# A transformer block: half of the MLP's gated column groups multiplied by GpSimd in one instruction instead of by VectorE in four

## The reference, cut to what matters

```python
h = _ln(x) * (1 + sc_msa) + sh_msa
x = x + _self_attn(h, ...) * g_msa                # stage A: windows of 128 rows, 16 heads
h = _ln(x) * (1 + sc_mca) + sh_mca
x = x + _topk_cross_attn(h, context, ...) * g_mca # stage B: the best 16 of 77 keys
h = _ln(x) * (1 + sc_mlp) + sh_mlp
u = h @ w_m1 + b_m1                               # stage C: the MLP, HID = 1024
a, b = (u[..., :HID], u[..., HID:])
x = x + (jax.nn.silu(a) * b @ w_m2 + b_m2) * g_mlp
# stage D: adaptive layer norm, cross-attention over 77 keys, residual
```

## Time and profile before

| | us |
|---|---|
| median of 3 runs | 997.29 |
| lowest and highest run | 996.76, 1002.76 |
| profiled execution, whole | 996.91 |
| its span, first to last instruction | 994.8 |
| busy in the span: PE | 945.2 |
| PE weight loads | 828.5 |
| DVE | 852.7 |
| ACT | 783.6 |
| POOL | 682.9 |

### The profile page before, as it was taken

The page is one execution under the profiler, slowest core; times in us unless marked ns, Lnnn a source line. Parts: engine busy times, 40 slices in busy tenths (PEclk is TensorE's granted clock), DMA queues, the critical chain, the costliest instruction groups (busy, mean ns, idle before and its releaser), DMA issues. The chain is left out here.

```text
span 994.8 us, 32865 instructions
## 1 busy us (share of the span) xinstructions
PE 945.2 (95%) x10750; PEld 828.5 (83%) x10750; DVE 852.7 (86%) x4268; ACT 783.6 (79%) x1679; POOL 682.9 (69%) x1099
## 2 busy tenths in 40 slices
PE   6876999999999999999999999999999999998896
PEld 4655888888889899888888999988898999877784
DVE  2599898999999999999999999999999998888544
ACT  2456788888888888888888888888888888776664
POOL 1347677777777777777777777777777776766843
PEclk9999999999999999999999999999999999999999
DMA  8474200000000011100000001000100000000000
GB/s 285 119 152 74 60 18 18 23 24 23 23 18 12 18 24 23 24 23 24 23 18 12 19 24 23 23 23 23 24 8 21 20 23 18 18 8 7 7 6 18
DMA packets 72154, 33.67 MB, mean 34 GB/s; under 512 B 56520, under 2 KB 68961, under 8 KB 71346
## 3 DMA queue, kind: packets, MB, share of 16 engines
q1 hardware_dynamic: 71986, 31.57, 12.9%
HBM read 22.64 MB, written 8.91 MB: 32 GB/s over the span
## 5 line engine op out<-in xcount | busy, mean ns | idle before, releaser
L2245 PE MATMUL ps<-hT_C,w_m_sb 128*128 128x128 f32 x2048 | 266.1, 279 | 1.4 <-DVE hidden_C L1584 0.6
L2245 PEld LDWEIGHTS ps<-hT_C,w_m_sb 128*128 128x128 f32 x2048 | 248.4, 192 | 15.0 <-issue 8.6
L960 ACT ACTIVATE silu_C<-ps,cols_sb 128x128 f32<-128x128 f32 x256 | 93.6, 368 | 77.4 <-PE ps L2245 75.8
L2256 PE MATMUL ps<-w_m_sb,hidden_C 128*128 128x256 f32 x512 | 120.8, 379 | 0.0
L617 POOL TENSOR_TENSOR p_B<-p_B,rc_B 128x616 f32<-128x616 f32 x64 | 79.5, 1243 | 53.2 <-DVE p_B L1498 48.3
L1490 DVE MATCH_REPLACE8 scores_left_B<-mx_B,scores_left_B 128x77 f32<-128x77 f32 x512 | 107.7, 223 | 0.0
L1486 DVE MATCH_REPLACE8 scores_left_B<-mx_B,scores_B 128x77 f32<-128x77 f32 x512 | 107.3, 225 | 0.0
L2256 PEld LDWEIGHTS ps<-w_m_sb,hidden_C 128*128 128x128 f32 x512 | 92.5, 190 | 10.0
L1584 DVE SCALAR_TENSOR_TENSOR hidden_C<-ps,cols_sb,silu_C 128x128 f32<-128x128 f32 x256 | 83.4, 336 | 14.8 <-ACT silu_C L960 14.5
L1438 DVE TENSOR_REDUCE mx_A<-ps 128x8 f32<-128x1024 f32 x64 | 75.3, 1219 | 19.4 <-PE ps L2150 19.4
L617 POOL TENSOR_TENSOR p_D<-scores_D,rc_D 128x616 f32<-128x616 f32 x63 | 77.1, 1226 | 21.3 <-DVE rc_D L1535 15.2
(11 more groups left out here) (187 smaller groups left out, 2499.6 us busy)
## 6 DMA issues: line engine op xcount, KB each, us to landing
xn_turned<-xn_blocks_A SPq DMA_DIRECT2D x124, 32.0 KB, 2.0
xn_A<-xn_turned SPq DMA_DIRECT2D x31, 128.0 KB, 2.1
x_A<-in_x SPq DMA_DIRECT2D x28, 128.0 KB, 2.4
out<-y_D SPq DMA_DIRECT2D x28, 128.0 KB, 2.3
w_m_sb<-in_w_m SPq DMA_DIRECT2D x3, 1024.0 KB, 5.8
w_mod_sb<-in_w_mod SPq DMA_DIRECT2D x2, 1024.0 KB, 9.9
gate_b<-row_tables SPq DMA_DIRECT2D x3, 512.0 KB, 4.6
gate<-row_tables SPq DMA_DIRECT2D x2, 512.0 KB, 3.9
```

The costliest lines, as they stand in the source:

```text
L960: sc.activation(SA[:, j, :], bank(f"C.up{j}")[:, 0:P], ACT.Silu, bias=col("bm1_a", j)).then_inc(sa_ok, 1)
L2245: ins = mm(bank(f"C.up{j}")[:, half * P:(half + 1) * P], w_m1[:, k, m:m + P], HT["C"][:, t % HT_COPIES["C"], k, :], start=(k == 0), stop=( ...
L2256: ins = mm(bank("C.dn0")[:, 0:CH], G[:, t % G_COPIES, j, :], w_m2[:, j, :], start=(j == 0), stop=(j == HJ - 1))
```

## The change: what it does

Groups 0 to 3 (`DIRECT = HJ // 2`) stay as they are. For groups 4 to 7:

- the four `hidden` steps on DVE go, in fill, body and drain;
- ACT does one more instruction behind each of silu 4 to 7: an Identity activation that reads the b half from the same PSUM bank, adds its bias and writes it to a new tile UB in SBUF (4 x 128 columns, one copy); this instruction now releases the bank;
- POOL does one product SA * UB of 512 columns per tile (`multiply_rest`), which waits for all eight silus and all four copies, and whose semaphore `gp_ok` is what `down(t, 1)` now waits for. In the body it stands between `less_max` of D half 0 and `reciprocal_root` of B;
- silu 4 to 7 of the next tile wait for this product, as it reads SA and UB.

The steps that move the input of stage A through DRAM (`move_input`, `turn_input`) are rewritten so that they could serve other stages too. With `TURNED = {"A": range(1, 32)}` they issue the same transfers with the same waits, in the same place.

```diff
+DIRECT = HJ // 2
+TURNED = {"A": range(1, 32)}
+        UB = sb("gate_half_C", [P, HJ - DIRECT, P])
...
+            def multiply_rest(t):
+                pool.wait_ge(sa_ok, HJ * t + HJ)
+                pool.wait_ge(ub_ok, (HJ - DIRECT) * (t + 1))
+                if first(t):
+                    pool.wait_ge(wo_done, 2)
+                    pool.wait_ge(ct_ps, 1)
+                if t >= G_COPIES:
+                    pool.wait_ge(y_ps["C"], t + 1 - G_COPIES)
+                g.tensor_tensor(G[:, t % G_COPIES, DIRECT:, :], SA[:, DIRECT:, :], UB[:], ALU.mult).then_inc(gp_ok, 1)
...
                 run(less_max, i, 6, "D", 0)
+                run(multiply_rest, i, 5)
                 run(reciprocal_root, i, 2, "B")
                 run(less_max, i, 6, "D", 1)
...
             def silu(t, j):
                 act.wait_ge(u_ps, HJ * t + j + 1)
                 if not first(t):
-                    act.wait_ge(g_ok, HJ * (t - 1) + j + 1)
+                    if j < DIRECT:
+                        act.wait_ge(g_ok, DIRECT * (t - 1) + j + 1)
+                    else:
+                        act.wait_ge(gp_ok, t)
                 sc.activation(SA[:, j, :], bank(f"C.up{j}")[:, 0:P], ACT.Silu, bias=col("bm1_a", j)).then_inc(sa_ok, 1)
+                if j >= DIRECT:
+                    sc.activation(UB[:, j - DIRECT, :], bank(f"C.up{j}")[:, P:2 * P], ACT.Identity, bias=col("bm1_b", j)).then_inc(ub_ok, 1)
...
-                run(hidden, i, 6, 4)
                 run(select, i, 4, 3, 2)
                 run(select, i, 4, 1, 2)
-                run(hidden, i, 6, 5)
                 run(select, i, 4, 2, 3)
                 run(residual, i, 3, "A")
-                run(hidden, i, 6, 6)
                 run(statistics, i, 3, "B")
-                run(hidden, i, 6, 7)
...
-                claim(BANK[f"C.up{j}"], (g_ok, HJ * t + j + 1))
+                if j < DIRECT:
+                    claim(BANK[f"C.up{j}"], (g_ok, DIRECT * t + j + 1))
+                else:
+                    claim(BANK[f"C.up{j}"], (ub_ok, (HJ - DIRECT) * t + j - DIRECT + 1))
...
-                pe.wait_ge(g_ok, HJ * t + (half + 1) * HJ // 2)
+                if half == 0:
+                    pe.wait_ge(g_ok, DIRECT * (t + 1))
+                else:
+                    pe.wait_ge(gp_ok, t + 1)
```

More of the change, by code:

```diff
@@ L139, in block_kernel @@
         attention_work("A")
-        XB = sb("xn_blocks_A", [P, CH])
+        XB = {s: sb(f"xn_blocks_{s}", [P, CH]) for s in TURNED}
         KBa = sb("kblk_A", [P, KC, 2, P])
@@ L293, in last, with by_transfer, transfers, transposed @@
             return t == TILES - 1
+        def by_transfer(t, s):
+            return t in TURNED.get(s, ())
+        def transfers(t, s):
+            return sum(by_transfer(u, s) for u in range(t))
+        def transposed(t, s):
+            return t - transfers(t, s)
         def place(t, name):
@@ L849, in normalise @@
                 if not first(t):
-                    if s == "A":
-                        act.wait_ge(h_ok["A"], t)
+                    if by_transfer(t - 1, s):
+                        act.wait_ge(h_ok[s], t)
                     else:
-                        act.wait_ge(h_ps[s], t)
+                        act.wait_ge(h_ps[s], transposed(t, s))
                 sc.activation(XN[s][:], X[s][:, t % X_COPIES, :], ACT.Identity, scale=RS[s][:], bias=NM[s][:]).then_inc(xn_ok[s], 1)
             def modulate(t, s):
-                by_transfer = s == "A" and not first(t)
-                if by_transfer:
-                    act.wait_ge(xt_in, 16 * t)
+                if by_transfer(t, s):
+                    act.wait_ge(xt_in[s], 16 * (transfers(t, s) + 1))
                 else:
-                    act.wait_ge(h_ps[s], t + 1)
+                    act.wait_ge(h_ps[s], transposed(t, s) + 1)
                 if first(t):
@@ L1424, in statistics, with turn_input @@
                 v.bn_aggr(MV[s][:], ST[s][:, t % 2, :]).then_inc(stats[s], 1)
-            def turn_input(t):
-                dve.wait_ge(xn_ok["A"], t + 1)
-                if t > 1:
-                    dve.wait_ge(xb_out, 16 * ROWS * (t - 1))
-                v.transpose(XB[:], XN["A"][:]).then_inc(xb_ok, 1)
+            def turn_input(t, s):
+                if not by_transfer(t, s):
+                    return
+                dve.wait_ge(xn_ok[s], t + 1)
+                n = transfers(t, s)
+                if n > 0:
+                    dve.wait_ge(xb_out[s], 16 * ROWS * n)
+                v.transpose(XB[s][:], XN[s][:]).then_inc(xb_ok[s], 1)
             def maxima_a(t, c):
@@ L1702, in fill @@
                 select(2, 3, 2)
-                hidden(0, 4)
                 residual(3, "A")
                 statistics(3, "B")
-                hidden(0, 5)
-                hidden(0, 6)
                 select(2, 0, 2)
@@ L1710, in fill @@
                 select(2, 0, 3)
-                hidden(0, 7)
                 keep_chosen(2, 0)
@@ L1830, in drain @@
                 hidden(TILES - 6, 3)
-                hidden(TILES - 6, 4)
                 select(TILES - 4, 3, 3)
-                hidden(TILES - 6, 5)
                 statistics(TILES - 5, "C")
@@ L1871, in drain @@
                 hidden(TILES - 5, 3)
-                hidden(TILES - 5, 4)
                 select(TILES - 3, 3, 0)
-                hidden(TILES - 5, 5)
                 select(TILES - 3, 3, 1)
@@ L1915, in drain @@
                 statistics(TILES - 3, "C")
-                hidden(TILES - 4, 4)
                 turn_back(TILES - 1)
```

98 lines of the change are left out of this document (49 added, 49 removed).

## The result

The changed kernel is slower: 1006.22 us in the median of its 44 executions (fastest 1001.29), the kernel before 999.64 us in 139 executions beside it and beside the experiments, on five chips (fastest 996.17). The first comparison, 20 executions of each, gave a ratio of 1.0074 with a 95% interval of [1.0051, 1.0096] (medians 1006.68 and 1000.01); two later ones gave 1.0060 [1.0033, 1.0087] and 1.0054 [1.0026, 1.0082]. I had forecast 998.1 with a range of 993.0 to 1003.5; the median of the first comparison lies 3.2 us above the range, that of all 44 executions 2.7.

What follows compares the result with a forecast made beforehand. PE was taken to bound the steady part, with waits on other engines at the ends. Steady 0, fill -0.5 and drain +1.3 gave +0.8 us on 997.29, so 998.1 us, range 993 to 1003.5.

Steps and rivals of the forecast that it cites:

- What bounds the kernel: Steady part, 155 to 852 us: PE has no gap, so time taken off DVE there buys nothing by itself.
- faster throughout: Rival: PE's smooth record hides waits on DVE and the kernel follows DVE; -24 us, 973; chance 0.02.
- Banks: each of groups 4 to 7 ... Cost 0: Steady tile: ACT instead of DVE reads these banks, 0.26 us behind the silu start; up 6 and 7 get no wait.
- fall into waits for the next up: Steady tile, ACT: copies 4 and 5, 0.26 us of queue each, use time in which ACT waits anyway.
- The bound of 0.3 us a tile: Steady part: forecast cost 0, between 0 and 0.3 us a tile.
- ACT's cover: Steady tile: table load moves 0.51 us later, just covered by 0.52 us idle before key_blocks; cost 0, bounds 0 and 0.1.
- product: POOL's 512-column product: 1.28 us, bounds 0.87 and 1.55; ends 0.3 us before down half 1's weight loads; cost 0 to 0.3.
- collision: Steady tile: keep_chosen on DVE waits for the product, then reciprocal_root on POOL may wait 0.8 us for keep_chosen.
- PE sees none of it: Steady tile: add_residual moves from 508.92 to 509.3 us, POOL's next idle time takes this up, and PE loses nothing.
- The wait of 0.80 us on the maxima: Fill: PE waits for DVE's maxima behind hidden 4 to 7 of tile 0; 1.0 us less queue removes it, -0.8.
- By some 0.3 us: Fill, tile 1: the product pushes POOL's gapless chain to its weights for B; +0.3 us.
- Larger waits ... take most of it in: Drain, tiles 28 and 29: product ends 0.3 to 0.4 us late, mostly absorbed by waits for other engines; +0.2 us.

Runs made afterwards that it cites:

- e7: Kernel before without VectorE's products of groups 4 to 7, given to no other engine; median 996.92 us, ratio 0.9967.
- e4: The change in tiles 27 to 31 alone, other tiles as in the kernel before; +1.6 ± 0.8 us over the kernel before at the same clock.
- e3: The change in tiles 0 to 2 alone, other tiles as in the kernel before; +1.3 ± 0.8 us over the kernel before at the same clock.
- e2: The change in tiles 3 to 26 alone, other tiles as in the kernel before; +1.9 ± 0.8 us over the kernel before at the same clock.
- e6: Kernel before plus a 512-column GpSimd product of silu values with themselves, read by nobody; +2.0 ± 0.8 us over the kernel before at the same clock.
- e1: Changed kernel with copy 4 moved behind weights_t(D, 1) in the body; first median 1001.81 us, +4.3 ± 0.6 us over the kernel before at the same clock.

## Why the prediction was wrong, point by point

**What bounds the kernel** was right. PE sets the steady part; e7 removes 1.0 us of DVE's queue in every tile and the repeat stays at 28.08. The rival "faster throughout" did not happen.

**Steady part, predicted 0, measured +2.05 us.** The step that failed is "Banks: each of groups 4 to 7 ... Cost 0". It asked what the copies do to the banks of up 4 to 7 and not what they do to the bank that ACT releases next on its queue, bank 5, which project_o of A waits for. Bank 5 had been released in time for project_o with nothing to spare: 0.09 us later on ACT was 0.08 us later on PE, in every tile. That copies 4 and 5 "fall into waits for the next up" was true of silu 5 and not of weights_t(D, 1) in between. The bound of 0.3 us a tile did hold this value, but by another cause, a late product or copy 7; and 27 tiles of it would have been 8 us, of which the range took up only 5, at a chance of 0.10.

**ACT's cover** held: key_blocks had 0.52 us of idle time, the delay was given as 0.51, and the changed kernel leaves it 0.16 us in the body tiles, so the delay was 0.36. The **product** was sized well, 1268 ns, and no body tile waits for it. The **collision** came as told in the body. Timeline of POOL, the changed kernel run again:

```profile
540.40 1.27 POOL L657 TENSOR_TENSOR hidden_C<-silu_C,gate_half_C 128x512 f32<-128x512 f32 x1 [0.29 <-issue]
541.63 0.75 POOL L563 TENSOR_TENSOR ve_B<-mv_B,eps 128x1 f32<-128x1 f32 x1
...
544.61 0.73 POOL L667 TENSOR_TENSOR x_D<-xg_C,tmp_C 128x256 f32<-128x256 f32 x1
```

reciprocal_root's first step takes 0.75 us where it takes 0.19 elsewhere, while keep_chosen runs on DVE until 542.33:

```profile
541.14 1.19 DVE L1554 SCALAR_TENSOR_TENSOR p_B<-scores_left_B,p_B 128x616 f32<-128x616 f32 x1
```

Add_residual has lost its 1.80 us of idle time without anyone waiting for it. In this tile the two engines' steps follow each other as in the Trainium skill's account of the shared port pair (SBUF — State Buffer, "SBUF: two separate sides").

"PE sees none of it" was true of the body and not of tile 0, where the same two steps met the other way round, the product 0.09 us behind keep_chosen, so that the product ended 0.56 us later than with its usual 1.27 us. That is up to 0.56 of the 0.76 us that PE waited; no run parts the two.

**Start, predicted -0.5, measured +1.3.** Of this 0.57 us is the product of tile 0, for which the prediction had no term: it asked when POOL's product comes in body tiles, in tile 1 and in the drain. The other 0.7 lies between tile 0 and tile 3. The wait of 0.80 us on the maxima did not go away, it fell to 0.49, and gated of tile 1 does come 0.9 us sooner (25.96 for 26.85 us after tile 0), though down of that tile only 0.3 us sooner on PE. All of it is given back by the next tile, in two waits of 0.47 and 0.52 us for the weights of B on GpSimd, where before there was one of 0.19 us; GpSimd had no slack. Then the product of tile 1 pushes reciprocal_root of B: neg_mean_B ends 1.4 us later, and PE waits 0.46 us for xn_B. "By some 0.3 us" was the other mis-sized term, and a gain of DVE's was counted as one of PE's without asking whether GpSimd could follow.

**End and tail, predicted +1.3, measured +2.7** (e4 against e3, tile by tile; against e2, whose clock was full in tile 28 to 29, it would be +2.9):

| tile | predicted | measured, by gated | measured, by the start of down half 1 on PE |
|---|---|---|---|
| 27 | -0.45 | -0.39 | +0.21 |
| 28 and 29 | +0.2 | +0.73 + 0.20 | +0.03 + 0.77 |
| 30 | +0.6 | +0.66 | +0.09 |
| 31 | +0.95 | +0.96 | +0.95 |
| tail | 0 | +0.51 | |

By gated, three of the five terms are right to 0.06 us, but two of these owe that to the marker. In tiles 27 and 29 of e3 gated does not wait for PE: in tile 27 it stands behind other work of DVE and begins 0.6 us after PE has finished its input. That wait goes in e4, and the -0.39 is this, while PE comes 0.21 us later. The wait of 1.31 us from which the -0.45 was worked out lies after gated of tile 27 and fell to 1.02, so the size of that term is right by luck. In tile 30 the product sets half 1 of down 2.28 us behind half 0 instead of 1.73, which is the +0.6 that was told, and PE has got 0.46 back ahead of it. Tile 31 is right by both markers. The two terms that failed have one cause. I asked only who reads the product; what stood behind it on GpSimd's queue (reciprocal_root of B in tile 28, less_max half 1 in the tail) is read by ACT: it came 0.6 us late in tile 28, and in the tail ACT waited 0.95 us longer for it. ACT's own queue passed both on to PE. "Larger waits ... take most of it in" was not so, since the largest of them hang on that same queue.

Together: +2.05 in the steady part, +1.8 at the start and +1.3 to +1.6 at the end and tail beyond what was forecast, 5.1 to 5.4 us, where the level has 5.7 - 0.8 = 4.9 (4.5 to 5.3).

The median of 1006.2 is 8.1 us over the forecast of 998.1, some 3 us more than the level accounts for. Of these, 1 us goes with the clock, and 2.3 us is the base: I added +0.8 to 997.29, the median of three runs, and 139 executions of the same kernel have a median of 999.64. With that base the forecast would have been 1000.4, still 5.8 us short.

## What to carry to other kernels

When an instruction is put into a queue, follow the release of every buffer by the instructions right behind it, not only the buffers that it touches itself: on the bounding engine 0.08 us a tile is 2 us a kernel. A busy share of 99.9% and an empty list of waits don't exclude such a loss; compare the repeat of one step to 0.01 us and the distance between neighbours on the bounding engine. Relief of an engine that isn't the bound counts only where its consumer is idle and the other queues on that path have slack, and here those places were worth 3 to 4 us in all. And two steps that slow each other must be looked at in every stage: the body had room for their meeting, tile 0 had none.

## What the runs showed of the hardware that I had not expected

PE's timeline closes over a wait of 0.08 us: 695.09 to 696.66 us busy of 697 in both kernels, with 2 us difference in time. A product of 512 columns on GpSimd took 1.27 us from two tiles (the changed kernel) and 1.04 us from one tile with itself (e6).

The granted clock falls in different stretches in each execution of one kernel: 0.50 at 25 us in one of the changed kernel, 0.83 from 40 to 60 us and again from 915 to 925 us in one of e1. What it costs depends on where it falls: the stretch of 0.91 to 0.92 between 905 and 925 us cost the kernel before 0.5 to 0.8 us (27.75 us against 27.21 and 26.95), while the changed kernel run again had 0.84 from 915 to 925 us, where PE was busy 7.55 of 10 us, and has 27.40 us from tile 28 to 29, the same as in its third profile at 1.00. That place recurs: leaving out the first profile of the changed kernel, the clock was low between the gated steps of tiles 28 and 29 in 12 of 15 profiles, and at 1.00 in those of e1, e2 and the changed kernel's third.
